# Near tables of an attention kernel moved in parts of five and three tiles, with the split of the row maxima placed earlier on GpSimd

## The chip, the cores and the metric

One core of a Trainium2 chip runs the whole program as one launch. The metric is the device time of one execution in microseconds; the number before is the median of three executions. A profile of one further execution gives the engines' instructions in time. TensorE (PE) does the matrix products and transposes, VectorE (DVE) and ScalarE (ACT) read its results, GpSimd (POOL) works on tables in on-chip memory, and SyncE (SP) issues most transfers.

## What is computed

A layer of attention with relative positions, followed by a mixture of eight experts, on 4 sequences of 1024 tokens with 256 features. Attention has 16 heads of 16 features. Cut to what matters:

```python
scores = jnp.einsum('bhqd,bhkd->bhqk', q, k) / scale
c2p = jnp.take_along_axis(c2p_att, c2p_pos, axis=-1)        # q against the position rows, chosen by q - k
p2c = jnp.swapaxes(jnp.take_along_axis(p2c_att, p2c_pos, axis=-1), -1, -2)   # k against them
scores = scores + (c2p + p2c) / scale
probs = jax.nn.softmax(scores, axis=-1)
ctx = jnp.einsum('bhqk,bhkd->bhqd', probs, v)
```

The chosen position depends on q - k alone and is constant once they are 128 or more apart. So only a band of three 128-wide blocks around the diagonal needs a gather; the rest is a constant per row.

## The kernel before

Five stages follow each other: `spread` and `project` prepare tables and projections, `attend` does attention, `mix` the output projection and the routing, `experts` the expert layers. The change lies in `attend`.

`attend` runs over 64 units `n` (one head of one sequence), each of eight query tiles `t` of 128 rows; `s = 8 n + t` counts tiles. For each unit TensorE makes eight position tables (`make_table`), 16 tiles ahead of the scores; ScalarE copies each out of PSUM (`keep_table`, L859). A diagonal has to become a row: SyncE writes the tables to a scratch tensor in HBM (`skew_write`, L655) and reads them back with a row pitch that is one element shorter (`skew_read`, L665, one transfer for each of the two tables). Both happen in two parts. The write's parts are tiles 0 to 3 and 4 to 7; the read's parts are tiles 0 to 2 and 3 to 7 (`PIECES`). The result is `near`. GpSimd then fills in the ends of the band in five steps a part (`edge`, steps 0 to 4, L926, L929, L934, L939, L942), over `EDGES`, three and four tiles, with two small columns that `keep_side` copies (L914). When step 4 is done, it raises `near_made`.

TensorE's `score` makes the scores of a tile and adds the transposed `near` (L740), after waiting for the part that the tile needs. VectorE's `look` takes the row maximum (L814, L818, L825) and `level` (L833) subtracts it from the band. After the eighth tile GpSimd splits the eight row maxima into three bfloat16 terms (`split_top`, five small steps, L952 to L962), TensorE turns them (`turn_top`, L785), ScalarE copies them (L877) and sends them into the operand of the flipped scores. `flip` makes the transposed scores 13 tiles later, ScalarE takes their exponential (L865), and `weigh` (L777) sums with the values.

The order on every engine is written out by hand and kept in program order. SyncE's loop over `u` issues the second part's read of unit u + 1, the first part's write of u + 2, the loads of u + 4, the store of u - 2, the first part's read of u + 2 and the second part's write of u + 2; before each it waits on constants. GpSimd's order follows from the table `steps`: an entry (at, h, of) places the edge steps `of` of part h at the tile `at` of the loop, and `split_top(u)` follows the entries of tile 7. TensorE calls `turn_top` after the scores of tile 1 of the next unit, and everything behind it on TensorE waits for the split.

Of the kernel before, what the change touches and what calls it, by code (L numbers as in the profile page):

```python
# [16 lines left out]
P = 128  # L17
# [4 lines left out]
N = B * H  # L22
QT = S // P
# [7 lines left out]
BAND = 2 * P - 1  # L31
# [116 lines left out]
def view(t, offset, dims):  # L148

    return bass.AP(tensor=t, offset=offset, ap=dims)  # L150
# [404 lines left out]
def attend(nc, sem, spent, c_masks, split_d, far_d, v_d, pick_d, skew_d, ctx_d):  # L555
# [9 lines left out]
    SPOT = 2 * P  # L565
    TABLE = QT * SPOT
    PITCH = 2 * TABLE
    PIECES = ((0, 3), (3, QT))
    EDGES = ((0, 3), (3, QT - 1))
    TS = N * QT  # L570
    COLUMNS = [([0], [1, 2, 3], [4, 5, 6, 7]), ([0, 1], [2, 3], [4, 5, 6, 7]), ([1, 2], [3, 4], [0], [5, 6, 7]),
               ([2, 3], [4, 5], [0, 1], [6, 7]), ([3, 4], [5, 6], [0, 1, 2], [7]), ([4, 5], [6, 7], [0, 1, 2, 3]),
# [1 line left out]
    with ExitStack() as ctx:  # L574
        def sb(name, shape, dt=F32):
            return ctx.enter_context(nc.sbuf_tensor("t_" + name, shape, dt))
# [7 lines left out]
        quest, after, before = ([sb(f"{w}{i}", [ROWS, S], BF16) for i in range(BUFS)] for w in ("quest", "after", "before"))  # L584
        rows = sb("rows", [KROWS, H, 2, 2 * P], BF16)
        vals = [sb(f"vals{i}", [P, QT, VROW]) for i in range(2)]
        table = [sb(f"table{i}", [P, 2, 2, 4, SPOT]) for i in range(2)]
        side = [sb(f"side{i}", [P, 2, QT]) for i in range(2)]
        near = [sb(f"near{i}", [P, 2, QT, W3]) for i in range(2)]
        band = [sb(f"band{i}", [P, QT, W3]) for i in range(2)]  # L590
# [9 lines left out]
        table_ps = ps("table_ps", [P, 2, 2 * P])  # L600
# [27 lines left out]
        @block.sync  # L628
        def _(sp):
            part, far = N * DH * S, PARTS * S  # L630

            def load_unit(n):
                i = n % BUFS
                if n >= BUFS:
                    sp.wait_ge(flipped, 2 * QT * (n - BUFS + 1))
                for dst, side_at in ((after[i], TERMS * part), (quest[i], 0)):
                    sp.dma_start(dst[0:KROWS, :], view(split_d, side_at + n * (DH * S), [[part, TERMS], [S, DH], [1, S]])
                                 ).then_inc(hats_in[i], 16)
                for dst, far_at, many in ((quest[i][FAR:FAR + 6, :], n * (2 * far), 2 * PARTS),
                                          (after[i][KROWS:FAR, :], (N + n) * (2 * far) + far, PARTS),  # L640
                                          (before[i][KROWS:FAR, :], (N + n) * (2 * far), PARTS)):
                    sp.dma_start(dst, view(far_d, far_at, [[S, many], [1, S]])).then_inc(hats_in[i], 16)

            def load_vals(b):
                if b >= 2:
                    sp.wait_ge(summed, QT * BATCH * (b - 1))
                sp.dma_start(vals[b % 2][:, :, :], view(v_d, b * (S * VROW), [[VROW, P], [P * VROW, QT], [1, VROW]])
                             ).then_inc(vals_in[b % 2], 16)

            def skew_write(n, h):  # L650
                sp.wait_ge(table_kept, n * QT + 4 * h + 4)
                if n >= 2:
                    sp.wait_ge(skew_in[n % 2][0], 16 * 2 * (n // 2))
                    sp.wait_ge(skew_in[n % 2][1], 16 * 2 * (n // 2))
                sp.dma_start(view(skew_d, n % 2 * (P * PITCH) + h * 4 * SPOT + 1, [[PITCH, P], [TABLE, 2], [1, 4 * SPOT]]),  # L655
                             table[n % 2][:, h, :, :, :].rearrange("p a u v -> p a (u v)")).then_inc(skew_out[n % 2][h], 16)

            def skew_read(n, h):
                if n >= 2:
                    sp.wait_ge(scored, (n - 2) * QT + 4 * h + 4)  # L660
                    sp.wait_ge(seen, (n - 2) * QT + 4 * h + 4)
                sp.wait_ge(skew_out[n % 2][h], 16 * (n // 2 + 1))
                lo, hi = PIECES[h]
                for tab in range(2):
                    sp.dma_start(near[n % 2][:, tab, lo:hi, P:W3],  # L665
                                 view(skew_d, n % 2 * (P * PITCH) + tab * TABLE + lo * SPOT + P,
                                      [[PITCH - 1, P], [SPOT, hi - lo], [1, SPOT]])).then_inc(skew_in[n % 2][h], 16)

            def store(n):
                sp.wait_ge(sum_kept, n + 1)  # L670
                sp.dma_start(view(ctx_d, n * (P * 2 * P), [[2 * P, P], [1, 2 * P]]), made[n % 2][:, :]
                             ).then_inc(ctx_out[n % 2], 16)

            for semaphore in spent:
                sp.sem_clear(semaphore)
            sp.dma_start(rows[:, :, :, :].rearrange("p h a v -> p (h a v)"), pick_d[:, :]).then_inc(rows_in, 16)
            for u in range(-4, N + 3):
                if 0 <= u + 1 < N:
                    skew_read(u + 1, 1)
                if 0 <= u + 2 < N:  # L680
                    skew_write(u + 2, 0)
                if 0 <= u + 4 < N:
                    load_unit(u + 4)
                if u == -4:
                    sp.dma_start(masks[:, :, :], c_masks).then_inc(const_in, 16)
                if 0 <= u - 2 < N:
                    store(u - 2)
                if u == -4:
                    load_vals(0)
                if u % BATCH == 4 and u // BATCH + 1 < B:  # L690
                    load_vals(u // BATCH + 1)
                if 0 <= u + 2 < N:
                    skew_read(u + 2, 0)
                if 0 <= u + 2 < N:
                    skew_write(u + 2, 1)
            for i in range(2):
                sp.wait_ge(ctx_out[i], 16 * (N // 2))

        @block.tensor
        def _(pe):  # L700
# [16 lines left out]
            def score(s):  # L717
                n, t = s // QT, s % QT
                i, out = n % BUFS, scores_ps[s % 2]
                if s >= 2:  # L720
                    pe.wait_ge(seen, s - 1)
                if s == 0:
                    pe.wait_ge(const_in, 16)
                    pe.wait_ge(ident_made, 1)
                if t == 0 and n < BUFS:
                    pe.wait_ge(rows_set[n], 16 * 3)
                if t == 0:
                    pe.wait_ge(twin_made, n + 1)
                at = 0
                for piece in COLUMNS[t]:  # L730
                    size = len(piece) * P
                    keys = after[i] if piece[0] <= t else before[i]
                    nc.tensor.matmul(out[:, at:at + size], quest[i][0:XROWS, t * P:(t + 1) * P],  # L733
                                     keys[0:XROWS, piece[0] * P:piece[0] * P + size],
                                     start=at % 512 == 0, stop=(at >= 512 and at + size == S), skip_group_check=True)
                    at += size
                pe.wait_ge(near_made, n * 2 + (1 if t < 3 else 2))
                lo, hi = band_of(t)
                for j in range(lo, hi):
                    last = nc.tensor.matmul(out[:, (j - lo) * P:(j - lo + 1) * P],  # L740
                                            near[n % 2][:, 1, j, (t - j + 1) * P:(t - j + 2) * P], ident,
                                            start=False, stop=(j == hi - 1), is_transpose=True, skip_group_check=True)
                last.then_inc(scored, 1)
# [62 lines left out]
        def _(dve):  # L806
            def look(s):
# [4 lines left out]
                out = scores_ps[c]  # L812
                dve.wait_ge(scored, s + 1)
                nc.vector.tensor_reduce(most[:, c, 1:2], out[:, wide:S], AX.X, ALU.max)  # L814
                dve.wait_ge(near_made, n * 2 + (1 if t < 3 else 2))
                if n >= 2:
                    dve.wait_ge(flipped, 2 * ((n - 2) * QT + min(t + 1, QT - 1)) + 2)
                nc.vector.tensor_tensor_reduce(band[n % 2][:, t, 0:wide], out[:, 0:wide],  # L818
# [32 lines left out]
        def _(act):  # L851
            def keep_table(x):
                n, u = x // QT, x % QT
                h = u // 4
                act.wait_ge(table_made, x + 1)
                if u % 4 == 0 and n >= 2:
                    act.wait_ge(skew_out[n % 2][h], 16 * (n // 2))
                    act.wait_ge(side_kept, (n - 2) * 2 + h + 1)
                nc.scalar.copy(table[n % 2][:, h, :, u % 4, :], table_ps[:, :, :]).then_inc(table_kept, 1)  # L859

            def exponent(s, half):
                act.wait_ge(flipped, 2 * s + half + 1)
# [45 lines left out]
        @block.gpsimd  # L908
        def _(pool):
            def keep_side(n, h):  # L910
                pool.wait_ge(table_kept, n * QT + 4 * h + 4)
                if n >= 2:
                    pool.wait_ge(edge_made, (n - 2) * 10 + (5 if h == 0 else 10))
                nc.gpsimd.tensor_copy(side[n % 2][:, :, 4 * h:4 * h + 4], table[n % 2][:, h, :, :, BAND]).then_inc(side_kept, 1)  # L914

            def edge(n, h, step):
                i = n % 2
# [29 lines left out]
            def split_top(n):  # L947
                i, done = n % 2, 5 * n
                if n >= 2:
# [11 lines left out]
                pool.wait_ge(split_made, done + 4)  # L961
                nc.gpsimd.tensor_copy(top_part[i][:, 2, :], top_rest[:, 1, :]).then_inc(split_made, 1)  # L962

            steps = ((2, 0, (0, 1)), (3, 0, (2,)), (4, 0, (3,)), (5, 0, (4,)),
                     (6, 1, (0, 1)), (7, 1, (2,)), (8, 1, (3,)), (9, 1, (4,)))
            nc.gpsimd.memset(before_rows[:, :], -1.0).then_inc(before_set, 1)
            pool.wait_ge(before_set, 1)
            nc.gpsimd.memset(before_rows[0:6, :], 0.0).then_inc(before_set, 1)
# [3 lines left out]
            for s in range(-AHEAD, TS):  # L972
                u, t = s // QT, s % QT
                if t == 0 and 0 <= u + 1 < N:
                    keep_side(u + 1, 1)
                if t == 4 and 0 <= u + 2 < N:
                    keep_side(u + 2, 0)
                for at, h, of in steps:
                    n = (s - at) // QT + 1
# [660 lines left out]
```

## Time and profile before

| | |
|---|---|
| three executions | 1993.77, 1996.8, 2002.08 us |
| median | 1996.8 us |
| the profiled execution | 2003.63 us |
| its span, first to last instruction | 2001.7 us |
| mean granted clock of TensorE | 0.916 |
| busy: TensorE, VectorE, ScalarE, GpSimd | 85%, 68%, 56%, 53% of the span |
| attention stage, roughly | 215 to 1500 us |

A share of busy time is an average over five stages that differ; it says little about any one of them. The times below are microseconds from the start of the span. Idle time stands in square brackets, with the engine and the line that ended it. "SPq" is SyncE's issue of a transfer, not the transfer itself.

### The profile page before, as it was taken

Reading aid. Unit: us, or ns where it says so; the run is one execution under the profiler, and the core shown is the slowest. Engines: PE = TensorE matmul, PEld = TensorE weight load, DVE = VectorE, ACT = ScalarE, POOL = GpSimd, SP = SyncE. Lnnn points to the kernel's source line nnn. Section 1 sums busy time; section 2 is a strip of 40 time slices with the busy share of each in tenths; the row PEclk is TensorE's granted clock in tenths of the full one; section 3 lists DMA queues with packets and bytes.
Section 4 is the critical chain, followed back from the end, with each engine's and each line's share of the span. In section 5 each row is a group of like instructions: output and inputs, shape, how many; then the busy total and the mean of one; then the engine's idle time right before and its main releaser. Section 6 shows DMA issues by size and latency. Waiting matters only on the chain. (4 is left out here: it accounts for less than half of the span.)

```text
span 2001.7 us, 40568 instructions
## 1 busy us (share of the span) xinstructions
PE 1698.0 (85%) x13688; PEld 1159.6 (58%) x13688; DVE 1370.7 (68%) x3938; ACT 1121.8 (56%) x2233; POOL 1069.1 (53%) x1268
## 2 busy tenths in 40 slices
PE   1882389999999999999999999999973674999997
PEld 1451156565656566566565666566532464999996
DVE  1673188788888788898798899899843553343343
ACT  1672257676767677677677777677751460222221
POOL 0210267676777667667576777777711451233332
PEclk6996589999999999999999999999996675999998
DMA  4598778777777777777877777787718852676772
GB/s 113 188 303 274 225 250 262 246 237 251 245 261 248 256 247 240 257 254 245 265 237 251 249 261 250 240 272 246 235 44 215 284 176 86 198 212 215 223 219 78
DMA packets 320826, 453.36 MB, mean 226 GB/s; under 512 B 35132, under 2 KB 260303, under 8 KB 320526
## 3 DMA queue, kind: packets, MB, share of 16 engines
q1 hardware_dynamic: 308034, 415.25, 65.2%
q10 hardware_dynamic: 7596, 21.10, 3.4%
q0 software_dynamic: 4992, 14.43, 1.9%
q8 instruction: 112, 1.84, 0.4%
q14 instruction: 92, 0.75, 0.1%
HBM read 257.32 MB, written 193.65 MB: 225 GB/s over the span
## 5 line engine op out<-in xcount | busy, mean ns | idle before, releaser
L865 ACT ACTIVATE t_probsT<-t_flip 128x512 f32<-128x512 f32 x1024 | 619.2, 607 | 242.7 <-PE t_flip L756 117.5
L814 DVE TENSOR_REDUCE t_most<-t_scores 128x1 f32<-128x640 f32 (+1 forms) x512 | 436.7, 853 | 169.8 <-PE t_scores L740 166.5
L833 DVE TENSOR_SCALAR t_band<-t_band,t_top 128x384 f32<-128x384 f32 (+1 forms) x512 | 383.8, 750 | 0.0
L859 ACT COPY t_table<-t_table_ps 128x512 f32<-128x512 f32 x512 | 298.2, 582 | 70.7 <-issue 41.1
L777 PE MATMUL t_sum_ps<-t_probsT,t_vals 128*32 128x256 f32 x4096 | 329.5, 394 | 0.2 <-ACT t_probsT L865 0.2
L926 POOL TENSOR_TENSOR t_near<-t_near,t_masks 128x384 f32<-128x384 f32 (+1 forms) x128 | 146.8, 1147 | 338.9 <-DMA t_near<-skew_d 336.4
L942 POOL TENSOR_TENSOR t_near<-t_near,t_masks 128x768 f32<-128x768 f32 (+1 forms) x128 | 272.4, 2129 | 0.0
L763 PE MATMUL t_flip<-t_masks,t_band 128*128 128x128 f32 x1408 | 263.0, 276 | 0.0
L818 DVE CUSTOM_DVE_ANT_0 t_band<-t_scores,t_near 128x384 f32<-128x384 f32 (+1 forms) x512 | 262.1, 512 | 0.0
L740 PE MATMUL t_scores<-t_masks,t_near 128*128 128x128 f32 x1408 | 243.5, 277 | 7.1 <-POOLq L945 7.1
L733 PE MATMUL t_scores<-t_after,t_quest 105*128 105x256 bf16 (+3 forms) x1024 | 244.9, 289 | 2.6 <-DVE t_most L818 2.4
L740 PEld LDWEIGHTS t_scores<-t_masks,t_near 128*128 128x128 f32 x1408 | 182.7, 143 | 46.6 <-POOLq L945 8.7
L712 PE MATMUL t_table_ps<-t_rows,t_quest 96*128 96x256 bf16 x512 | 143.5, 280 | 69.1 <-DMA t_before<-far_d 49.8
L733 PE MATMUL t_scores<-t_before,t_quest 105*128 105x256 bf16 (+3 forms) x768 | 195.0, 294 | 0.0
L763 PEld LDWEIGHTS t_flip<-t_masks,t_band 128*128 128x128 f32 x1408 | 164.7, 143 | 4.8
L756 PE MATMUL t_flip<-t_quest,t_before 108*128 108x512 bf16 (+3 forms) x512 | 161.4, 316 | 0.8 <-ACT t_probsT L865 0.7
L756 PE MATMUL t_flip<-t_quest,t_after 108*128 108x512 bf16 (+3 forms) x512 | 158.7, 310 | 1.2 <-DMA t_quest<-t_topT 0.8
L1606 PE MATMUL e_hid_ps<-e_xT,e_w 128*128 128x128 f32 x1248 | 148.0, 278 | 5.6 <-DMA e_total<-total_d 5.2
L1606 PEld LDWEIGHTS e_hid_ps<-e_xT,e_w 128*128 128x128 f32 x1248 | 147.5, 194 | 8.2 <-issue 5.5
L939 POOL TENSOR_TENSOR t_near<-t_near,t_masks 128x384 f32<-128x384 f32 (+1 forms) x128 | 145.5, 1137 | 0.0
L714 PE MATMUL t_table_ps<-t_rows,t_after 96*128 96x256 bf16 x512 | 142.9, 279 | 0.0
L1588 PE MATMUL e_out_ps<-w_all,e_hid 128*128 x624 | 141.0, 379 | 0.0
(186 smaller groups left out, 2343.7 us busy)
## 6 DMA issues: line engine op xcount, KB each, us to landing
skew_d<-t_table SPq DMA_DIRECT2D x128, 1024.0 KB, 8.9
t_near<-skew_d SPq DMA_DIRECT2D x128, 640.0 KB, 6.2
t_near<-skew_d SPq DMA_DIRECT2D x128, 384.0 KB, 4.8
e_w<-in_L_ffn_W_dram ACTq DMA_DIRECT2D x39, 512.0 KB
e_w<-in_L_ffn_W_dram SPq DMA_DIRECT2D x39, 512.0 KB
split_d<-p_part SPq DMA_DIRECT2D x32, 384.0 KB
t_after<-split_d SPq DMA_DIRECT2D x64, 192.0 KB
t_quest<-split_d SPq DMA_DIRECT2D x64, 192.0 KB
```

Of the source, the lines that this page charges most:

```text
L733: nc.tensor.matmul(out[:, at:at + size], quest[i][0:XROWS, t * P:(t + 1) * P], keys[0:XROWS, piece[0] * P:piece[0] * P + size], start=at % ...
L740: last = nc.tensor.matmul(out[:, (j - lo) * P:(j - lo + 1) * P], near[n % 2][:, 1, j, (t - j + 1) * P:(t - j + 2) * P], ident, start=False ...
L756: last = nc.tensor.matmul(out[:, (a - lo) * P:(z - lo) * P], keys[:, j * P:(j + 1) * P], quest[i][:, a * P:z * P], start=first, stop=False ...
L763: last = nc.tensor.matmul(out[:, (t - lo) * P:(t - lo + 1) * P], band[n % 2][:, t, at:at + P], ident, start=False, stop=True, is_transpose ...
L777: last = nc.tensor.matmul(sum_ps[32 * g:32 * g + 32, 0:2 * P], vals[b % 2][:, j, h * VDIM:h * VDIM + 32], probsT[s % 3][:, g * 2 * P:(g + ...
L814: nc.vector.tensor_reduce(most[:, c, 1:2], out[:, wide:S], AX.X, ALU.max)
L818: nc.vector.tensor_tensor_reduce(band[n % 2][:, t, 0:wide], out[:, 0:wide], near[n % 2][:, 0, t, at:at + wide], 1.0, -3.0e38, ALU.add, ALU ...
L833: nc.vector.tensor_scalar(band[n % 2][:, t, 0:wide], band[n % 2][:, t, 0:wide], top[n % 2][:, t:t + 1], None, ALU.subtract).then_inc(level ...
L859: nc.scalar.copy(table[n % 2][:, h, :, u % 4, :], table_ps[:, :, :]).then_inc(table_kept, 1)
L865: nc.scalar.activation(probsT[s % 3][:, half * 512:(half + 1) * 512], flip_ps[half][:, :], ACT.Exp, scale=SCALE).then_inc(expd, 1)
L942: nc.gpsimd.tensor_tensor(tail, tail, masks[:, 1, :].unsqueeze(1).unsqueeze(1).to_broadcast([P, 2, many, P]), ALU.mult).then_inc(edge_made, 1)
L1606: last = nc.tensor.matmul(hid_ps[s % 2][:, c, :], w1[s % WB][:, f, c * P:(c + 1) * P], xT[s % 2][:, f, :], start=(f == 0), stop=(f == 1))
```

## The change

The tables of a unit are laid out as eight tiles in a row, not in two halves. They are written in parts of five and three tiles (`TILES`); the skewed read takes four and four (`PIECES`), and the edges four and three (`EDGES`). The waits follow: tiles 0 to 3 need the first part of `near`, tiles 4 to 7 the second, and the first write waits for five kept tables. `keep_side` of the first part moves from tile 4 to tile 5. In GpSimd's order the first part's steps move one tile later, steps 0 and 1 of the second part come at tile 7, directly ahead of `split_top`, and its steps 2, 3 and 4 come behind it; before, steps 0, 1 and 2 stood ahead of the split.

```diff
+    TILES = ((0, 5), (5, QT))
-    PIECES = ((0, 3), (3, QT))
-    EDGES = ((0, 3), (3, QT - 1))
+    PIECES = ((0, 4), (4, QT))
+    EDGES = ((0, 4), (4, QT - 1))
...
-        table = [sb(f"table{i}", [P, 2, 2, 4, SPOT]) for i in range(2)]
+        table = [sb(f"table{i}", [P, 2, QT, SPOT]) for i in range(2)]
...
             def skew_write(n, h):
-                sp.wait_ge(table_kept, n * QT + 4 * h + 4)
+                lo, hi = TILES[h]
+                sp.wait_ge(table_kept, n * QT + hi)
...
-                sp.dma_start(view(skew_d, n % 2 * (P * PITCH) + h * 4 * SPOT + 1, [[PITCH, P], [TABLE, 2], [1, 4 * SPOT]]),
-                             table[n % 2][:, h, :, :, :].rearrange("p a u v -> p a (u v)")).then_inc(skew_out[n % 2][h], 16)
+                sp.dma_start(view(skew_d, n % 2 * (P * PITCH) + lo * SPOT + 1, [[PITCH, P], [TABLE, 2], [1, (hi - lo) * SPOT]]),
+                             table[n % 2][:, :, lo:hi, :].rearrange("p a u v -> p a (u v)")).then_inc(skew_out[n % 2][h], 16)
...
             def skew_read(n, h):
                 if n >= 2:
-                    sp.wait_ge(scored, (n - 2) * QT + 4 * h + 4)
-                    sp.wait_ge(seen, (n - 2) * QT + 4 * h + 4)
+                    sp.wait_ge(scored, (n - 2) * QT + TILES[h][1])
+                    sp.wait_ge(seen, (n - 2) * QT + TILES[h][1])
...
-                pe.wait_ge(near_made, n * 2 + (1 if t < 3 else 2))
+                pe.wait_ge(near_made, n * 2 + (1 if t < 4 else 2))
...
-                dve.wait_ge(near_made, n * 2 + (1 if t < 3 else 2))
+                dve.wait_ge(near_made, n * 2 + (1 if t < 4 else 2))
...
             def keep_table(x):
-                h = u // 4
+                h = 0 if u < TILES[0][1] else 1
...
-                if u % 4 == 0 and n >= 2:
+                if u == TILES[h][0] and n >= 2:
...
-                nc.scalar.copy(table[n % 2][:, h, :, u % 4, :], table_ps[:, :, :]).then_inc(table_kept, 1)
+                nc.scalar.copy(table[n % 2][:, :, u, :], table_ps[:, :, :]).then_inc(table_kept, 1)
...
             def keep_side(n, h):
-                pool.wait_ge(table_kept, n * QT + 4 * h + 4)
+                lo, hi = TILES[h]
+                pool.wait_ge(table_kept, n * QT + hi)
                 if n >= 2:
-                    pool.wait_ge(edge_made, (n - 2) * 10 + (5 if h == 0 else 10))
-                nc.gpsimd.tensor_copy(side[n % 2][:, :, 4 * h:4 * h + 4], table[n % 2][:, h, :, :, BAND]).then_inc(side_kept, 1)
+                    pool.wait_ge(edge_made, (n - 2) * 10 + 10)
+                nc.gpsimd.tensor_copy(side[n % 2][:, :, lo:hi], table[n % 2][:, :, lo:hi, BAND]).then_inc(side_kept, 1)
...
-            steps = ((2, 0, (0, 1)), (3, 0, (2,)), (4, 0, (3,)), (5, 0, (4,)),
-                     (6, 1, (0, 1)), (7, 1, (2,)), (8, 1, (3,)), (9, 1, (4,)))
+            steps = ((3, 0, (0, 1)), (4, 0, (2,)), (5, 0, (3,)), (6, 0, (4,)), (7, 1, (0, 1)), (8, 1, (2, 3)), (9, 1, (4,)))
...
-                if t == 4 and 0 <= u + 2 < N:
+                if t == 5 and 0 <= u + 2 < N:
                     keep_side(u + 2, 0)
```

## Rows read from the trace of the kernel before

**Rows 1.** Windows: stretch, busy us of each engine, PEclk, DMA share, GB/s.

```profile
262.00:1440.00 1178.00, 1119.69 (x10259) 705.44 (x10259) 1022.47 (x2930) 853.51 (x1639) 841.18 (x1043) 0.98 0.77 250
```

**Rows 2.** Waits of SyncE's queue: us in total, times, longest us.

```profile
SPq L662 <- DMA skew_d<-t_table: 726.6, 120, 8.3
...
SPq L655 <- ACT t_table L859: 11.3, 11, 6.9
```

**Rows 3.** Timeline of SyncE, one unit: start us, us of issue.

```profile
1125.93 0.93 SPq L665 DMA_DIRECT2D t_near<-skew_d  x2
1126.96 0.56 SPq L655 DMA_DIRECT2D skew_d<-t_table  x1
...
1136.72 0.91 SPq L665 DMA_DIRECT2D t_near<-skew_d  x2
1137.74 0.57 SPq L655 DMA_DIRECT2D skew_d<-t_table  x1
...
1144.80 0.93 SPq L665 DMA_DIRECT2D t_near<-skew_d  x2
```

**Rows 4.** Transfers issued near 1127 and near 1138 us: KB, us to landing.

```profile
skew_d<-t_table SPq DMA_DIRECT2D x1, 1024.0 KB, 9.7
t_near<-skew_d SPq DMA_DIRECT2D x1, 640.0 KB, 7.1
...
skew_d<-t_table SPq DMA_DIRECT2D x1, 1024.0 KB, 7.0
t_near<-skew_d SPq DMA_DIRECT2D x1, 384.0 KB, 5.0
```

**Rows 5.** The line of the table's writes: first and last start us.

```profile
L655 SPq DMA_DIRECT2D skew_d<-t_table x128: 525/567/1772, 221.1 to 1439.8; - x128
```

**Rows 6.** Windows of 1 us inside the unit (last number: GB/s).

```profile
1129.90:1130.90 1.00, 1.00 (x14) 0.51 (x13) 0.97 (x6) 0.55 (x2) 0.00 (x0) 1.00 0.72 225
1132.90:1133.90 1.00, 1.00 (x10) 0.86 (x9) 0.96 (x6) 0.65 (x2) 0.41 (x1) 1.00 1.01 409
```

**Rows 7.** Timeline of GpSimd, same unit.

```profile
1133.49 1.27 POOL L926 TENSOR_TENSOR t_near<-t_near,t_masks 128x512 f32<-128x512 f32 x1 [4.63 <-DMA t_near<-skew_d]
...
1136.82 0.25 POOL L952 CAST t_top_part<-t_top 128x8 bf16<-128x8 f32 x1
...
1137.95 0.19 POOL L962 CAST t_top_part<-t_top_rest 128x8 bf16<-128x8 f32 x1
...
1142.19 1.00 POOL L926 TENSOR_TENSOR t_near<-t_near,t_masks 128x384 f32<-128x384 f32 x1 [0.31 <-DMA t_near<-skew_d]
...
1143.93 0.83 POOL L934 TENSOR_TENSOR t_near<-t_near,t_side 128x384 f32<-128x384 f32 x1
1144.70 0.32 POOL L914 COPY t_side<-t_table 128x8 f32<-128x8 f32 x1
...
1145.96 1.81 POOL L942 TENSOR_TENSOR t_near<-t_near,t_masks 128x768 f32<-128x768 f32 x1
```

**Rows 8.** Timeline of TensorE: `near` at tile 0, then `turn_top`.

```profile
1133.98 0.38 PE L740 MATMUL t_scores<-t_masks,t_near 128*128 128x128 f32 x2
...
1138.20 0.23 PE L785 MATMUL t_table_ps<-t_ident,t_top_part 128*24 128x128 bf16 x1 [1.00 <-POOL t_top_part L962]
```

**Rows 9.** Waits between 300 and 1440 us: total, times, longest.

```profile
DVE t_most L814 <- PE t_scores L740: 130.1, 210, 6.7
...
ACT t_topT L877 <- PE t_table_ps L785: 75.8, 59, 5.0
```

**Rows 10.** Timeline of VectorE: `level` without and beside GpSimd's work.

```profile
1130.39 0.42 DVE L833 TENSOR_SCALAR t_band<-t_band,t_top 128x384 f32<-128x384 f32 x1
...
1133.87 1.11 DVE L833 TENSOR_SCALAR t_band<-t_band,t_top 128x384 f32<-128x384 f32 x1
```

**Rows 11.** Timeline of ScalarE: tables kept, at the start and in the unit.

```profile
220.46 0.58 ACT L859 COPY t_table<-t_table_ps 128x512 f32<-128x512 f32 x1 [0.70 <-PE t_table_ps L714]
...
1144.09 0.58 ACT L859 COPY t_table<-t_table_ps 128x512 f32<-128x512 f32 x1
```

## The prediction

> **What bounds the kernel now.** I read the windows by stage first: the attention stage, 262 to 1440 us of a span of 2001.7 us, has 1178 us, and all that the diff touches lies in it. TensorE is busy for 1120 us of it, VectorE for 1022, GpSimd for 841, and the DMA engines for 0.77 of it [rows 1]. No engine is full, so I looked at who waits for whom, on SyncE's queue first, because it issues every transfer of the near tables in a written order. It waits 726.6 us at L662, the wait of `skew_read` for the write of the same part, in 120 of 128 cases; for a table still missing (L655) it waits 11.3 us in 11 cases [rows 2]. SyncE's own timeline shows why. A unit (one head of one batch entry, eight query tiles) is one round of four transfers: read of the second part 1125.93, write of the next unit's first part 1126.96, then the loads and the store, read of that first part 1136.72, write of the second part 1137.74, and the next round begins at 1144.80 [rows 3]. The two writes need 9.7 and 7.0 us to land [rows 4]: 1126.96 + 9.7 = 1136.66 and 1137.74 + 7.0 = 1144.74, each 0.06 us before the read behind it is issued. So the round of 18.87 us is: write, wait until it has landed, read, next write. Nothing that TensorE, VectorE, ScalarE or GpSimd does in the unit stands in that round. The first and last write of all 128 stand at 221.1 and 1439.8 [rows 5]: 63 rounds and one half of 10.8 us, or 19.17 us a round on average. 63 x 19.17 = 1208 us is the whole stage.
>
> The windows of DMA traffic show that the transfers run in the order of issue: about 225 GB/s while the read of 1 KB rows is served, 409 when the write's turn comes [rows 6]. The second part's read had landed when GpSimd, which waited for it, took it at 1133.49; the write issued behind it landed 3.17 us later. In the other half the read landed by 1142.19 and the write 2.55 us later [rows 4, 7].
>
> Then I looked for TensorE's stall. `turn_top` (L785) sits idle for 1.00 us before 1138.20, released by the split's last step [rows 8]; between 300 and 1440 us ScalarE waits 75.8 us for that matmul, in 59 units, 1.28 us each [rows 9]. GpSimd's timeline says why it is late: it begins the second part when the read lands, 1133.49, does three steps of four tiles, then the split 1136.82 to 1138.14 [rows 7]. This stall is real, but it begins with the landing of a read, so with SyncE's round.
>
> **The change, step by step.** Lengths first. Each read is two transfers, of 640 or of 384 KB [rows 4]. The transfers of a unit were: long half, read 1280 KB and write 1024; short half, read 768 and write 1024. Now: long half, read 1024 and write 1280; short half, read 1024 and write 768. Each half keeps its total, 2304 and 1792 KB, and the number of issues and their order on SyncE are as before; loads, store and the `topT` transfer are untouched. 256 KB of write and 256 KB of read change places. Price of the read: the read landed 7.56 us after its first issue for 1280 KB (1125.93 to 1133.49) and 5.47 for 768 (1136.72 to 1142.19), 2.09 for 512 KB, so 1.05 for 256; if I put the whole difference of the two landings (9.7 - 7.0) down to the read it is 1.35. Price of the write: a quarter of 2.55 or of 3.17 us, so 0.64 to 0.79. With 1.05 and 0.70 the long half becomes 0.35 us shorter and the short half 0.35 longer: the round changes by 0. Bounds: if the price of a byte differs between the halves, in either direction by all it can, (1.35 - 1.05) + (0.79 - 0.64) = 0.45 us a round, 28 us in 63 rounds, both ways. I take 0, because what tells the two halves apart, the loads and the store issued behind the long half's write, stays as it is.
>
> GpSimd: seven tiles of edges a unit before and after, four and three in place of three and four, so its work stays. The split now has two steps of three tiles ahead of it: 1142.19 to 1143.93, 1.74 us, in place of 3.33 (1133.49 to 1136.82) [rows 7]. With the read landing 1.05 earlier the split ends 1.05 + 1.59 = 2.64 us earlier in the round, about 1135.50. Its data are there: VectorE began the work that follows the last row maximum at 1133.87 [rows 10], and the split would begin at 1134.18. Behind the split wait steps 2, 3 and 4 of the second part, 3.7 us (1143.93 to 1147.77 less a side copy), so ready at about 1139.2; they are wanted at tile 4, whose scores follow the table copy of 1144.09 [rows 11]. The first part's chain grows from three tiles to four: now 5.58 us with a side copy of 0.3 (1142.19 to 1145.96 + 1.81), so 5.28 x 4/3 + 0.3 = 7.3 us. Its read is 1.05 longer and is issued 0.35 earlier, so it runs from 1142.9 to 1150.2; tile 0 of the next unit wants it at 1133.98 + 18.87 = 1152.85. So TensorE can move forward by up to 2.64 us within the round, and no further, since tile 0 would then wait for the first part. Where does the stall go? Nowhere: TensorE has less work a unit (18.87 less 1.00) than SyncE's round, so it waits about as long, at `turn_top` again or at tile 0.
>
> New waits: the first write wants five tables instead of four; behind it on SyncE stand the loads, the store, the first part's read, for which GpSimd waits, and the next write. In the unit shown the fifth table is kept at 1144.09 + 0.58 = 1144.67 [rows 11], the write goes at 1145.83: 1.16 us to spare, plus what TensorE moves forward. Cost 0; without that cover it costs what the table is late. The first read wants one more tile scored; in the unit before, that tile follows the table of 1144.09 - 18.87 = 1125.2, 11 us ahead of the read at 1136.72, and VectorE needs a tile's time, some 2 us: cost 0.
>
> Ends: at the start tables come every 0.58 + 0.70 = 1.28 us [rows 11], so the first write goes 1.28 later and lands 0.7 later still; with the short half's 0.35 that is 2.3 us more by the last round. Behind the last read TensorE is 2.64 ahead. Sum: 0 x 63 + 2.3 - 2.6 = -0.3 us. The profiled execution took 2003.63 us (its span is 2001.7), so 2003.3; the median of the three runs is 6.8 below it, and from there I predict 1996.5 us. A change within 0.5% (10 us, 0.16 us a round) is about what a measurement of this kernel cannot tell from none.
>
> **The rivals.** (a) The stall on TensorE decides after all, because SyncE's wait has room that I don't see. Then the price is 63 times what ScalarE waits for it, 1.28 us [rows 9], 81 us, or 63 us by the 1.00 of the unit shown: 1916 to 1934. For it: the stall comes back in nearly every unit. Against it: the 0.06 us between a landing and the next issue. The Trainium skill's page Perfetto Trace Analysis (section What "DMA-bound" means) names busy DMA engines, a solid issuing queue or SBUF's reads as what a DMA-bound kernel is bound by; with 0.77 and gaps in the queue this stage is none of these, and by that rule (a) would hold. The trace does not agree that the list is whole: landings at 1136.66 and issues at 1136.72 are a queue bound by completions. Chance 0.09.
> (b) The halves trade unevenly in our favour, for instance because 768 KB land behind 1024 KB of read before the slowest engine is held up: up to -28 us, 1968. Chance 0.12. (c) The same against us, up to +28, 2025: chance 0.07.
> (d) The fifth table closes a loop, slower: write, landing 9.4, read 5.47 + 1.05, edges 7.3, tile 0 to the fifth table kept 10.7 (1133.98 to 1144.67), 33.9 us for two rounds, 37.7 us. It decides once these grow by 3.8 us; at 5 more it costs 0.6 a round, 38 us, 2035. Chance 0.04.
> (e) VectorE becomes the bound, slower. L833 takes 0.42 us with GpSimd idle and 1.11 beside it [rows 10], 0.69 more for each meeting. VectorE waits 130.1 us for scores between 300 and 1440 us [rows 9], 2.2 us a round (60 of them). Four more meetings a round would pass that by 0.56 us, 35 in all: 2032. GpSimd's work does not grow, only its place. The Trainium skill's page SBUF — State Buffer (section SBUF: two separate sides) says that the two engines share a port pair as an exclusive lock, so that the later one stands still; the 1.11 us agree, and by that rule too the cost follows meetings, not the order of steps. Chance 0.03.
>
> **How the numbers follow.** Forecast (round unchanged) 0.65, its own range 1987 to 2006. Faster by over 0.5%: (a) and (b), 0.21. Slower: (c), (d), (e), 0.14. (b) and (c) are spread from 10 to 28 us; cutting 4 us off their ends leaves out 0.03 more than (a), (d) and (e) with 0.16, so 1972 to 2021 holds 0.81.
>
> **What would show it.** Right: SyncE's round stays at 18.9 us, its long half 0.35 shorter, its short half 0.35 longer, with the wait at L662 (now some lines lower) still near 727 us; the split starts about 1.7 us behind the landed read instead of 3.3; the wait before `turn_top` shrinks only as far as another wait of TensorE grows. Wrong: a round under 18.6 us with the halves' landings shortened (b), a round that follows TensorE's work, near 17.9 us (a), waits of SyncE for tables (d), or VectorE without idle time (e).

## The result, and the profile after

The changed kernel takes 2070.14 us (median of 4 runs, 2065.28 to 2072.74) against 1998.8 us for the kernel before on the same chip: ratio 1.0356, 95% interval 1.0325 to 1.0387. It is slower by about 71 us, where no change was forecast and 2021 us was the upper end of the range.

The attention stage has become longer; TensorE's share of busy time over the span fell from 85% to 83%. First and last write of the tables, first and last start in microseconds, and the waits of SyncE's queue over the whole run (us in total, times, longest):

```profile
L657 SPq DMA_DIRECT2D skew_d<-t_table x128: 525/560/2167, 221.9 to 1509.7; - x128
```

```profile
SPq L664 <- DMA skew_d<-t_table: 790.4, 121, 8.7
...
SPq L657 <- ACT t_table L861: 13.7, 22, 7.9
```

From first to last write it is now 1287.8 us, before 1218.7 [rows 5]: 69.1 us more. The spans differ by just that, 2070.8 - 2001.7 = 69.1. So the whole loss lies in 63 rounds, 1.10 us in each. SyncE waits 64 us longer for writes to land (790.4 against 726.6) [rows 2], and hardly longer for tables. One ordinary round, SyncE's timeline (start us, us of issue), then the landings of its transfers (KB, us to landing; issues near 910, then near 921):

```profile
909.15 0.91 SPq L667 DMA_DIRECT2D t_near<-skew_d  x2
910.16 0.56 SPq L657 DMA_DIRECT2D skew_d<-t_table  x1
...
919.70 0.93 SPq L667 DMA_DIRECT2D t_near<-skew_d  x2
920.73 0.57 SPq L657 DMA_DIRECT2D skew_d<-t_table  x1
929.23 0.91 SPq L667 DMA_DIRECT2D t_near<-skew_d  x2
```

```profile
skew_d<-t_table SPq DMA_DIRECT2D x1, 1280.0 KB, 9.5
t_near<-skew_d SPq DMA_DIRECT2D x1, 512.0 KB, 6.2
...
skew_d<-t_table SPq DMA_DIRECT2D x1, 768.0 KB, 8.4
t_near<-skew_d SPq DMA_DIRECT2D x1, 512.0 KB, 6.4
```

The chain is the one of before: 910.16 + 9.5 = 919.66, the read goes at 919.70; 920.73 + 8.4 = 929.13, the read goes at 929.23. But the round has 20.08 us, not 18.87 [rows 3]. The long half's write lands 0.2 us sooner than before, the short half's write 1.4 us later [rows 4], although it carries a quarter less. GpSimd and TensorE in the same round:

```profile
915.82 1.00 POOL L929 TENSOR_TENSOR t_near<-t_near,t_masks 128x384 f32<-128x384 f32 x1 [1.98 <-DMA t_near<-skew_d]
...
917.55 0.25 POOL L955 CAST t_top_part<-t_top 128x8 bf16<-128x8 f32 x1
...
926.56 1.28 POOL L929 TENSOR_TENSOR t_near<-t_near,t_masks 128x512 f32<-128x512 f32 x1 [3.98 <-DMA t_near<-skew_d]
```

```profile
918.93 0.23 PE L787 MATMUL t_table_ps<-t_ident,t_top_part 128*24 128x128 bf16 x1 [0.94 <-POOL t_top_part L965]
```

The split starts 1.73 us behind the landed read, not 3.33 [rows 7]. TensorE waits for it all the same. Waits between 300 and 1440 us:

```profile
DVE t_most L816 <- PE t_scores L742: 175.9, 188, 5.4
ACT t_topT L879 <- PE t_table_ps L787: 109.1, 56, 4.7
```

Both have grown (130.1 and 75.8 before [rows 9]): the engines wait out a longer round.

For the comparison of kernels below I took from SyncE's and GpSimd's timelines, for about 55 rounds each (300 to 1400 us), the time from a half's first read to GpSimd's first step on it (the read's landing; only where GpSimd had waited for it) and from there to the next read (the write behind it). Medians in us; the last column is the mean round.

| kernel | long half: read, write behind | short half: read, write behind | round |
|---|---|---|---|
| before (reads 5, 3; writes 4, 4) | 7.43, 3.22 | 5.58, 2.67 | 19.31 |
| changed (reads 4, 4; writes 5, 3) | 6.87, 3.69 | 6.76, 2.53 | 20.39 |

A read of four tiles lands after 6.8 us in either half; the mean of three and five is 6.5. By the medians the reads account for +0.62 us a round, the writes behind them for +0.33; by the means, which add up to the round, it is +0.59 and +0.49, together the 1.08 of the last column. The two parts are not cleanly apart: in the changed kernel's short half the traffic, averaged over 53 rounds, is above 400 GB/s from 6.0 us after the first issue, and the read is complete only at 6.76, so part of the write is likely under way while the last of the read is still out.

### The profile page after: what moved, and what is told of

Same layout as the page of the kernel before. It is cut to its first block and busy times, and to the rows that moved or that the text cites. A ratio compares the mean times of both kernels' runs of the same rounds, so it can differ in the third digit from the quotient of the medians.

```text
span 2070.8 us, 40568 instructions
## 1 busy us (share of the span) xinstructions
PE 1726.3 (83%) x13688; PEld 1168.9 (56%) x13688; DVE 1385.7 (67%) x3938; ACT 1122.0 (54%) x2233; POOL 1069.4 (52%) x1268
## 5 line engine op out<-in xcount | busy, mean ns | idle before, releaser
L835 DVE TENSOR_SCALAR t_band<-t_band,t_top 128x384 f32<-128x384 f32 (+1 forms) x512 | 404.1, 789 | 0.0
L929 POOL TENSOR_TENSOR t_near<-t_near,t_masks 128x512 f32<-128x512 f32 (+1 forms) x128 | 147.0, 1148 | 407.6 <-DMA t_near<-skew_d 407.6
L779 PE MATMUL t_sum_ps<-t_probsT,t_vals 128*32 128x256 f32 x4096 | 334.1, 398 | 0.2 <-ACT t_probsT L867 0.2
L945 POOL TENSOR_TENSOR t_near<-t_near,t_masks 128x1024 f32<-128x1024 f32 (+1 forms) x128 | 270.7, 2115 | 0.0
L742 PE MATMUL t_scores<-t_masks,t_near 128*128 128x128 f32 x1408 | 249.7, 282 | 12.9 <-POOLq L948 12.6
L735 PE MATMUL t_scores<-t_before,t_quest 105*128 105x256 bf16 (+3 forms) x768 | 199.7, 300 | 0.0
L942 POOL TENSOR_TENSOR t_near<-t_near,t_masks 128x512 f32<-128x512 f32 (+1 forms) x128 | 147.2, 1150 | 0.0
```

The source lines that it names most:

```text
L779: last = nc.tensor.matmul(sum_ps[32 * g:32 * g + 32, 0:2 * P], vals[b % 2][:, j, h * VDIM:h * VDIM + 32], probsT[s % 3][:, g * 2 * P:(g + ...
L835: nc.vector.tensor_scalar(band[n % 2][:, t, 0:wide], band[n % 2][:, t, 0:wide], top[n % 2][:, t:t + 1], None, ALU.subtract).then_inc(level ...
L945: nc.gpsimd.tensor_tensor(tail, tail, masks[:, 1, :].unsqueeze(1).unsqueeze(1).to_broadcast([P, 2, many, P]), ALU.mult).then_inc(edge_made, 1)
```

## The experiments

Each ratio is to the kernel before on the same chip. The medians of that kernel lie between 1998.8 and 2014.1 us from chip to chip, so ratios from different chips can be set against each other only to about 0.8%.

**e1: GpSimd's order alone, on the old parts.**

```diff
-            steps = ((2, 0, (0, 1)), (3, 0, (2,)), (4, 0, (3,)), (5, 0, (4,)),
-                     (6, 1, (0, 1)), (7, 1, (2,)), (8, 1, (3,)), (9, 1, (4,)))
+            steps = ((3, 0, (0, 1)), (4, 0, (2,)), (5, 0, (3,)), (6, 0, (4,)), (7, 1, (0, 1)), (8, 1, (2, 3)), (9, 1, (4,)))
```

> GpSimd's new order on the old parts (writes 4 and 4, reads 3 and 5). Theory 1 (SyncE's round of writes and reads sets the pace, and only the transfers' sizes changed its length): the round stays at 19.1 us and the time at that of before within 8 us, although the split ends about 1 us earlier. Theory 2 (GpSimd's order lengthens the round by delaying TensorE or by meeting VectorE): 2060 us or more here.

2011.56 us, ratio 1.0038 (1.0015 to 1.0061). ScalarE's wait for the turned maxima fell by a third, between 300 and 1440 us:

```profile
ACT t_topT L877 <- PE t_table_ps L785: 48.4, 59, 4.4
```

27 us less waiting on TensorE's stall (75.8 before) and no gain: mean round 19.43, time 0.4% longer. The order is not the loss, and the stall it shortens was not the bound.

**e2: the new parts alone,** the changed kernel with the old `steps`.

> The new parts (writes 5 and 3, reads 4 and 4) with GpSimd's old order, three steps ahead of the split. Theory 1: as slow as the changed kernel, 2062 to 2078 us, round 20.4. Theory 2: back to about 2000 us.

2068.75 us, ratio 1.0340 (1.0320 to 1.0361), landings 6.82, 3.73, 6.74, 2.54, round 20.29. The parts carry the whole loss.

**e3: the new writes with the old reads.** The changed kernel with

```diff
-    PIECES = ((0, 4), (4, QT))
-    EDGES = ((0, 4), (4, QT - 1))
+    PIECES = ((0, 3), (3, QT))
+    EDGES = ((0, 3), (3, QT - 1))
```

and the waits of tile 3 as before.

> Writes of 5 and 3 tiles as in the changed kernel, reads of 3 and 5 as before, GpSimd's new order. Read theory (two reads of four tiles cost more than one of three and one of five, 13.6 against 13.0 us until they land): landings 5.6 and 7.4 as before, 1995 to 2022 us. Write theory (runs of 5 and 3 KB are written more slowly than runs of 4 KB): the writes land as late behind their reads as they do in the changed kernel or later, 2045 to 2080 us.

2008.88 us, ratio 1.0044 (1.0030 to 1.0058). The landings on the profile's page (medians over all). A write is one transfer. A read is two that raise one semaphore, and the page's median over both lies below the time at which the pair has landed:

```profile
skew_d<-t_table SPq DMA_DIRECT2D x64, 1280.0 KB, 10.0
t_near<-skew_d SPq DMA_DIRECT2D x128, 640.0 KB, 6.2
t_near<-skew_d SPq DMA_DIRECT2D x128, 384.0 KB, 4.6
skew_d<-t_table SPq DMA_DIRECT2D x64, 768.0 KB, 6.7
```

The same lines of the changed kernel:

```profile
t_near<-skew_d SPq DMA_DIRECT2D x256, 512.0 KB, 5.7
skew_d<-t_table SPq DMA_DIRECT2D x64, 1280.0 KB, 9.5
skew_d<-t_table SPq DMA_DIRECT2D x64, 768.0 KB, 8.2
```

The two writes take 10.0 + 6.7 = 16.7 us here, 9.5 + 8.2 = 17.7 in the changed kernel, with the same writes: 1.0 us a round, nearly the whole loss of 1.10. Writes of five and three tiles cost nothing extra; behind reads of three and five they land 3.59 and 2.34 us later, 5.93 in sum, against 5.89 before.

**e4: writes of 6 and 2, reads of 5 and 3** (`TILES` 6, `PIECES` and `EDGES` 5, waits moved along).

> Writes of 6 and 2 tiles, reads of 5 and 3, so each half again carries 2304 and 1792 KB; GpSimd's new order, edges five and two tiles. Read theory: the two reads land after 5.6 and 7.4 us again, whichever half they stand in, 1995 to 2025 us. Write theory: runs of 6 and 2 KB are no better than 5 and 3, 2060 us or more. A third theory (the short half pays more for a KB of read than the long half): its read has grown by another 256 KB, so slower than the changed kernel, 2100 us or more.

2002.47 us, ratio 0.9992 (0.9968 to 1.0015). Each half has the changed kernel's totals, the five-tile read merely stands in the other half, and the time is that of before. So it is not that a part grows or shrinks in the short half: with these rows, two reads of four are dear, a three and a five are not.

**e5 and e6: rows of the scratch tensor 17 KB apart,** on the kernel before and on the changed one.

```diff
-    PITCH = 2 * TABLE
+    PITCH = 2 * TABLE + SPOT
...
+                    for i in range(2):
+                        sp.dma_start(view(skew_d, i * (P * PITCH) + 2 * TABLE + 1, [[PITCH, P], [1, P]]), c_masks[:, 0, :]
+                                     ).then_inc(pad_out, 16)
```

> The kernel before with the rows of the scratch tensor 17 KB apart instead of 16 KB (256 elements of padding, filled once at the start from a constant). Pitch theory (the 16 engines' reads of 1 KB runs stand in each other's way because their rows are 16 KB apart): both reads may land earlier than 5.6 and 7.5 us, and the time falls. Count theory (the time to land is a bent function of the tiles read, 3, 4, 5, whatever the pitch): landings and time stay, 1995 to 2012 us.

> The changed kernel with the same padding. Pitch theory: the reads of four tiles land after 6.5 us or less instead of 6.8 (6.5 is the mean of three and five), so 0.6 us a round or more comes back: 2030 us or less. Count theory: landings of 6.8 us and 2062 to 2078 us again.

e5: 1981.64 us, ratio 0.9884 (0.9852 to 0.9915). e6: 2008.62 us, ratio 1.0032 (1.0015 to 1.0050); 61 us of the loss are gone. The two divisions are now 27 us apart instead of 71. e6's landings on the profile's page:

```profile
skew_d<-t_table SPq DMA_DIRECT2D x64, 1280.0 KB, 8.8
t_near<-skew_d SPq DMA_DIRECT2D x256, 512.0 KB, 5.6
skew_d<-t_table SPq DMA_DIRECT2D x64, 768.0 KB, 8.0
```

In the terms of the table above:

| kernel, rows 17 KB apart | long half: read, write behind | short half: read, write behind | round |
|---|---|---|---|
| e5 (reads 5, 3; writes 4, 4) | 7.11, 2.66 | 6.25, 2.63 | 18.99 |
| e6 (reads 4, 4; writes 5, 3) | 6.43, 3.29 | 6.83, 2.05 | 19.38 |

Both theories missed the form of it. In e6 the long half's read lands 0.44 us sooner than in the changed kernel and the short half's 0.07 later, and the writes behind them land 0.40 and 0.48 sooner (3.29 and 2.05 instead of 3.69 and 2.53). In e5 the read of five lands 0.3 us sooner than before, but the read of three 0.7 later. So with these rows two fours no longer cost more than a three and a five: 13.26 against 13.36 us (by the means 13.45 against 13.43). Of the 0.39 us a round between e5 and e6 the writes have 0.37 by the means. In windows of half a microsecond behind the short half's first issue, averaged over the 53 to 55 rounds between 300 and 1380 us, the changed kernel moves 239, 218 and 174 GB/s from 2.5 to 4 us, e6 moves 321, 301 and 243. The layout slows the stretch in which the read is served, and what stands behind it in the queue pays with it.

**e12: rows 32 KB apart, e13: the two buffers 33 KB further apart, e14: rows 64 bytes further apart,** all on the changed kernel.

In e12 the row distance is `4 * TABLE`, in e14 `2 * TABLE + 16` elements, filled as in e5. In e13 it stays, and the read (and likewise the write) becomes

```diff
-                                 view(skew_d, n % 2 * (P * PITCH) + tab * TABLE + lo * SPOT + P,
+                                 view(skew_d, n % 2 * (P * PITCH + 33 * SPOT) + tab * TABLE + lo * SPOT + P,
```

> The changed kernel with the rows of the scratch tensor 32 KB apart. Pitch theory (rows a power of two apart stand in each other's way): no better than at 16 KB, landings of 6.8 us or later, 2060 us or more. If any other layout than the old one had helped, it is like 17 KB: landings near 6.6, 2000 to 2020 us.

> The changed kernel, rows 16 KB apart as in it, but the two buffers of the scratch tensor 2 MB + 33 KB apart instead of 2 MB. If the slow reads come from a read of one buffer and a write of the other lying exactly 2 MB apart, this heals them as the spaced rows did: landings near 6.6, 2000 to 2020 us. If they come from the rows' own distance, nothing changes: 2060 us or more.

> The changed kernel with 16 elements (64 bytes) of padding a row, so rows 16 KB + 64 bytes apart. If the exact distance of 16 KB matters (skewed reads 16 KB less 4 bytes apart), a small shift heals: 2000 to 2020 us. If it is rows standing close to 16 KB apart at all, nothing changes: 2060 us or more. Somewhere between says that the shift from row to row counts by its size.

e12: 2007.86 us, ratio 0.9965 (0.9946 to 0.9984), mean round 19.40 like e6's 19.38. So a power of two as the distance is not the cause, and the pitch theory falls in that form. e13: 2068.14 us, ratio 1.0279 (1.0255 to 1.0304). The ratio is 0.8% under the changed kernel's, no more than chips differ by, and the mean round of 20.37 is the changed kernel's: the distance of the buffers is not it either. e14: 2032.84 us, ratio 1.0123 (1.0087 to 1.0160), mean round 19.67: some two thirds of the way to e6 (0.61 by time, 0.72 by ratio and by round). It is the rows standing 16 KB apart or very near it; what in the memory makes that slow, and why four tiles suffer more than three and five, stays open.

**e7: reads of 2 and 6 tiles** (`PIECES` and `EDGES` at 2, writes 4 and 4).

> Writes of 4 and 4 tiles as before, reads of 2 and 6 tiles, edges of two and five, GpSimd's new order. Only the landings decide here. Bent curve (each further tile costs less: 1.25 us for the fourth, 0.65 for the fifth): about 4.0 and 8.0 us, 12.0 in sum, less than the 13.0 of 3 and 5. Even counts are slow as such: over 13.3 in sum. Straight line with a bump at four alone: 4.6 and 8.4, 13.0.

2110.99 us in one run, because the second part of `near`, now wanted at tile 2, comes too late: between 300 and 1440 us TensorE waits 131.4 us, in 54 units, for GpSimd to raise `near_made`. SyncE's waits show another regime, so only the landings can be read:

```profile
SPq L655 <- ACT t_table L859: 397.4, 122, 6.9
SPq L662 <- DMA skew_d<-t_table: 320.1, 66, 8.5
```

```profile
t_near<-skew_d SPq DMA_DIRECT2D x128, 768.0 KB, 6.4
t_near<-skew_d SPq DMA_DIRECT2D x128, 256.0 KB, 3.5
```

The kernel before has these:

```profile
t_near<-skew_d SPq DMA_DIRECT2D x128, 640.0 KB, 6.2
t_near<-skew_d SPq DMA_DIRECT2D x128, 384.0 KB, 4.8
```

These medians bend: 3.5, 4.8, 5.7, 6.2, 6.4 us for two to six tiles (5.7 from the changed kernel). But they mix the two transfers of a pair (see e3). From the first issue until both have landed, as in the tables, it is 5.6, 6.8 and 7.4 us for three, four and five tiles: 1.2 us for the fourth, 0.6 for the fifth, and 13.6 for two fours against 13.0 for a three and a five. That is what the round pays at rows 16 KB apart. For two and six tiles the landings in e7's trace give 4.3 and 7.1. Six tiles sooner than five can't stand on one curve: in e7 the write behind a read goes out 3 to 6 us after it, in the other kernels 1 us after it. So e7 does not decide between a curve that bends all along and a price that reads of four alone pay. And e5 and e6 show that the curve is not one of the tile count alone: it depends on the rows' distance.

**e8 to e11: SyncE's round opened.** The second part's write goes out ahead of the first part's read, so it no longer waits for the first write.

```diff
-                if 0 <= u + 2 < N:
-                    skew_read(u + 2, 0)
                 if 0 <= u + 2 < N:
                     skew_write(u + 2, 1)
+                if 0 <= u + 2 < N:
+                    skew_read(u + 2, 0)
```

e8 has the old parts and GpSimd's new order, e9 is the changed kernel, e10 the kernel before, each with this edit alone; e11 is e8 with rows 17 KB apart.

> The old parts with GpSimd's new order, and on SyncE the second part's write issued ahead of the first part's read, so that it no longer waits for the first write to land. If SyncE's round of completions is what sets the pace, the round falls until TensorE's own work (about 17.9 us) or the tables hold it: 18.0 to 18.4 us, 1925 to 1955 us. If the pace is set by the bytes that the DMA engines move, the round stays at 19.1 and the time near 2000 us.

> The changed kernel (writes 5 and 3, reads 4 and 4) with the second write issued ahead of the first read on SyncE. If its loss comes only through SyncE's round of completions, the four-tile reads cost nothing once that round is opened: within 10 us of the old parts with the same early write, 1920 to 1940 us. If the slower reads load the DMA engines themselves, the distance of 60 to 70 us stays: 1985 to 2000.

> The kernel before, its own parts and GpSimd's own order, with the early write alone. If the earlier split had been hidden behind SyncE's round, it shows here: with the old order TensorE waits at its turn of the maxima by up to 1 us a unit, so 1935 to 1990 us, slower than 1929. If the old order is as good, 1925 to 1933 us.

> Old parts, GpSimd's new order, early write, and rows 17 KB apart. If TensorE, VectorE and the tables set the pace once the round is opened, faster reads are worth nothing: 1922 to 1935 us. If landings still count, another 10 to 20 us: 1905 to 1920.

e8: 1929.11 us, ratio 0.9635 (0.9618 to 0.9652). e9: 1942.06, ratio 0.9645 (0.9615 to 0.9676). e10: 1928.02, ratio 0.9573 (0.9543 to 0.9603). e11: 1930.71, ratio 0.9590 (0.9559 to 0.9621). In e8 SyncE waits for tables, and TensorE is busy for 1108 of 1118 us of the stage at a granted clock of 1.00 (windows; busy us by engine, clock, DMA share, GB/s):

```profile
SPq L655 <- ACT t_table L859: 311.9, 123, 6.6
SPq L662 <- DMA skew_d<-t_table: 219.0, 63, 5.9
```

```profile
262.00:1380.00 1118.00, 1108.21 (x10355) 705.65 (x10354) 1081.53 (x2953) 859.97 (x1651) 849.31 (x1046) 1.00 0.80 265
```

The DMA engines move more per microsecond than before (265 GB/s against 250 [rows 1]), so bytes were not the limit; the round of completions was. Of the 71 us of loss 14 remain between e9 and e10 on one chip, a little more than the 10 that were expected. Of the 12.5 us between the two profiled spans 3.1 stand ahead of the first write and 8.8 between the first and the last write; what makes those is not shown. Faster rows (e11) are worth nothing any more. And e10, with GpSimd's old order, is as fast as e8: the earlier split has no worth of its own even then. In e10, between 300 and 1440 us, GpSimd waits at the split for VectorE's row maxima in 61 units, although three steps of four tiles stand ahead of it:

```profile
POOL t_top_part L952 <- DVE t_peak L825: 168.3, 61, 11.1
```

e8, e10 and e11 lie within 3 us of one another. e10 needs the least: two statements changed places, 4.3% below the kernel before.

## Why the prediction was wrong

**The bound was named rightly.** SyncE's round of write, landing, read sets the pace: the loss of 69.1 us stands between the first and the last write to a tenth of a microsecond, and opening the round (e8, e10) gives 3.7 to 4.3%. Rival (a), that TensorE's stall decides, is refuted by e1: 27 us less stall, no gain.

**The step that failed** is "the round changes by 0", with its bounds of 0.45 us. Its term for 256 KB moved between the halves was mis-sized:

| term | predicted | measured (medians) |
|---|---|---|
| read, short half | +1.05 | +1.18 |
| read, long half | -1.05 | -0.56 |
| write behind it, long half | +0.70 | +0.47 |
| write behind it, short half | -0.70 | -0.14 |
| sum a round | 0 | +0.95 |

The medians leave 0.15 of the 1.10 us unplaced; by the means it is +0.59 for the reads and +0.49 for the writes. I had divided the difference between three and five tiles by two and taken the line as straight; the bounds let the price of a KB differ between the halves, but not between the fourth and the fifth tile. Three points were needed and two were there. The write's price failed too: the short half's write, a quarter smaller, was to give back 0.70 and gave 0.14. e3 and e4 show that what costs is two reads of four, and not the size of the writes or the half in which a read stands; why four are dear is open, and it hangs on the rows' distance of 16 KB, which the prediction left out. The loss is rival (c) in kind, more than twice as large as it allowed: 63 x 1.10 = 69 us instead of up to 28. The list of signs had none for it: a round that grows while SyncE still waits for writes alone. That the two divisions stand 27 us apart with spaced rows (e5, e6), near the bound of 28, is chance, because there the reads differ by next to nothing.

**GpSimd's part** came as worked out: 1.73 us from the landed read to the split (1.74 predicted), with the data there. (The three steps behind the split were put at 3.7 us; 1143.93 to 1147.77 less the side copy of 0.32 is 3.5, which changes nothing.) The stall did go nowhere; it grew with the round, as idle time of an engine that is not the bound does.

**The waits added** cost next to nothing, as forecast: SyncE waited 13.7 us for tables (11.3 before), so rival (d) did not come, and VectorE waited longer for scores than before, so nor did (e). The ends cancelled: the spans differ by what the rounds differ.

**The rule on what "DMA-bound" means.** The Trainium skill (Perfetto Trace Analysis, section What "DMA-bound" means) names three things that a DMA-bound kernel is bound on: specific DMA engines, the issuing engine's sequencer, and SBUF's read capacity. Taken as a whole list, it would have left the bound to TensorE's stall, rival (a). The measurement decides otherwise: the DMA engines were busy 0.77 of the stage, SyncE's queue had gaps, and the stage was still held by transfers, by their order of completion.

## What to carry to other kernels

When the pace is set by a queue that waits for each transfer to land, the time of a transfer has to be measured at the size and in the layout wanted: equal bytes in all did not mean equal time here, and with rows 16 KB apart two middle-sized reads cost more than a small and a large one. Before the pieces of such a chain are resized, look whether the chain can be opened: here issuing a write ahead of a read that it doesn't depend on gave 4%, and left the division of the parts worth 14 us instead of 71, layout and GpSimd's order worth nothing that could be measured. A stall on the busiest engine was worth nothing here while something outside it set the round; a kernel with that stall shortened and nothing else (e1) tells this in one run.

## What the runs showed of the hardware that was not expected

Rows of a scratch tensor 16 KB apart, written in runs of 3 to 5 KB and read back in runs of 1 KB at a pitch 4 bytes shorter, are slow to move: at 17 KB the kernel before gains 1.2% and the changed one 61 us, at 32 KB the changed one's round shrinks as much (20.39 to 19.40 us), at 16 KB + 64 bytes by some two thirds of that. In the changed kernel most of the gain shows in the writes queued behind the reads (3.69 to 3.29 and 2.53 to 2.05 us), and the rest in the long half's read (6.87 to 6.43); the short half's read lands no sooner.
